# A graph network's first stage: three multiplies for each chunk of edges go from DVE to POOL

## The reference

```
h  = relu(layernorm(x))
xp = h @ W0                               # 3125 x 1024, 4 heads of 256
a_src, a_dst = xp . att_src, xp . att_dst # per node and head
alpha = softmax over the edges of a node (and itself) of leaky_relu(a_src[src] + a_dst[dst])
x  = x + relu(sum over edges of alpha * xp[src] + bias)
h  = relu(layernorm(x));  h = h @ W1;  al = h . a_l;  ar = h . a_r
e  = exp(-leaky_relu(al[src] + ar[dst]))
out = x + elu(sum over edges, by src, of e * h[dst] / (sum of e + 1e-5))
```

## Time and profile before

| | us |
|---|---|
| median of 3 runs | 2025.16 (2017.92 to 2032.6) |
| the profiled execution, its time | 2027.11 |
| its span in the profile | 2025.0 |
| first stage: last scores copied | 503.6 |
| first instruction of the next stage | 513.2 |

### The profile page before, as it was taken

One profiled execution on the slowest core, in us unless ns is written; L12 is line 12 of the kernel. 1 busy time (PEld: TensorE's weight loads), 2 busy tenths in 40 slices (PEclk: granted clock), 3 DMA queues, 4 the chain that ended last, 5 costly groups with the idle time before them and its releaser, 6 DMA issues. The chain is left out here.

```text
span 2025.0 us, 27950 instructions
## 1 busy us (share of the span) xinstructions
PE 1583.1 (78%) x10493; PEld 837.8 (41%) x10493; DVE 1233.0 (61%) x2870; ACT 445.0 (22%) x768; POOL 1039.1 (51%) x1060
## 2 busy tenths in 40 slices
PE   3897999897168777777677676169999999999896
PEld 2444545443034344344344333014544544454454
DVE  4999999997147777777777877342333333333332
ACT  3332333221002221122211221021222221122121
POOL 1121212111656776767767650376666766666630
PEclk9897999998577787878878887569999999999898
DMA  7321333221889999999999983599999999999961
GB/s 234 93 93 57 87 93 96 85 94 48 348 304 347 381 362 382 369 374 381 379 376 373 380 330 113 206 410 352 365 360 359 352 363 355 344 370 349 330 213 47
DMA packets 170575, 554.44 MB, mean 274 GB/s; under 512 B 32195, under 2 KB 37178, under 8 KB 170080
## 3 DMA queue, kind: packets, MB, share of 16 engines
q0 software_dynamic: 128128, 417.93, 56.0%
q1 hardware_dynamic: 38708, 121.44, 17.4%
q10 hardware_dynamic: 3600, 13.24, 1.8%
HBM read 547.51 MB, written 53.52 MB: 297 GB/s over the span
## 5 line engine op out<-in xcount | busy, mean ns | idle before, releaser
L1064 POOL DMA_INDIRECT ring<-layer_rows,idx x360 | 394.4, 1096 | 188.3 <-issue 86.8
L1655 POOL DMA_INDIRECT ring<-layer_rows,idx x360 | 369.7, 1027 | 186.3 <-issue 94.8
L588 PE MATMUL mm<-w_sb,hT 128*128 128x512 f32 x800 | 362.6, 607 | 0.0
L1190 PE MATMUL acc<-ring,weight 128*32 128x256 f32 (+1 forms) x3600 | 334.6, 480 | 26.4 <-issue 14.3
L1717 PE MATMUL acc<-ring,weight 128*32 128x512 f32 x1600 | 221.3, 630 | 39.7 <-issue 34.5
L588 PEld LDWEIGHTS mm<-w_sb,hT 128*128 128x128 f32 x800 | 153.4, 197 | 174.7 <-issue 174.7
L1190 PEld LDWEIGHTS acc<-ring,weight 128*32 128x32 f32 (+1 forms) x3600 | 154.0, 137 | 155.3 <-issue 118.4
L1817 DVE TENSOR_TENSOR hT_low<-tp_l,hT_high 128x512 fp32r<-128x512 f32 x50 | 34.6, 692 | 300.3 <-issue 248.4
L467 POOL CAST row_l<-asd 128x4 bf16<-128x4 f32 x25 | 4.8, 190 | 336.9 <-DVE asd L677 336.9
L1750 PE MATMUL mm_l<-w_high,hT_high 128*128 128x512 f32 x400 | 169.1, 423 | 8.5 <-issue 6.0
L1752 PE MATMUL mm_l<-w_high,hT_low 128*128 128x512 f32 x400 | 163.4, 409 | 10.1 <-issue 10.0
(11 more groups left out here) (271 smaller groups left out, 2419.0 us busy)
## 6 DMA issues: line engine op xcount, KB each, us to landing
layer_rows<-row_l ACTq DMA_DIRECT2D x25, 517.0 KB
layer_rows<-row_l SPq DMA_DIRECT2D x25, 514.0 KB
own<-layer_rows SPq DMA_DIRECT2D x25, 512.0 KB
x<-xb SPq DMA_DIRECT2D x25, 512.0 KB
x1t<-x SPq DMA_DIRECT2D x25, 512.0 KB
xt<-in_x_dram SPq DMA_DIRECT2D x24, 512.0 KB
xb<-in_x_dram SPq DMA_DIRECT2D x24, 512.0 KB
out_dram<-y SPq DMA_DIRECT2D x24, 512.0 KB
```

The source lines that it names most:

```text
L588: last = pe.matmul(mm[k][:, f * HALF:(f + 1) * HALF], hT[k][:, c, :], w_sb[:, c, f * HALF:(f + 1) * HALF], start=c == 0, stop=c == KC - 1)
L1064: pool.indirect_dma_start(out=ring[:, t % 2, blocks(c), :][:, q, :], out_offset=None, in_=table0, in_offset=bass.IndirectOffsetOnAxis(ap=i ...
L1190: last = pe.matmul(acc[t % 2][k * n:(k + 1) * n, h, :], by[:, k, h, :], ring[:, t % 2, blocks(c), h * C:(h + 1) * C][:, k, :], start=c == ...
L1655: pool.indirect_dma_start(out=fetched(t, c)[:, q, :], out_offset=None, in_=table1, in_offset=bass.IndirectOffsetOnAxis(ap=idx, axis=0), bo ...
```

## The change

placed and the two halves of parts are multiplied by POOL. placed is POOL's place_ranks: it waits for the scan of the chunk (scanned) and, for the buffer, for PE's ranks of the chunk two before. The halves are POOL's spread_fields: it waits for at_spot of the chunk (a new semaphore, spotted). DVE, in turn, waits before at_spot until POOL has multiplied both halves of the chunk before (spread_done), since at_spot has one buffer; its waits for placed_done before mine and before the scan were there already and are now waits for POOL. Sizes, types and the results are the same.

```diff
@@ POOL's functions
+            def place_ranks(c):
+
+                pool.wait_ge(scanned, 3 * c + 1)
+                if c >= 2:
+                    pool.wait_ge(ranked, c - 1)
+                pool.tensor_tensor(placed[c % 2][:, :], running[:, :], mine[c % 2][:, :], ALU.mult)\
+                    .then_inc(placed_done, 1)
+
+            def spread_fields(c):
...
+                pool.wait_ge(spotted, c + 1)
+                then(pool.tensor_tensor(parts[k][:, :, 0, :], at_spot[:, :, :], along(high_T[:, cols]), ALU.mult),
+                     halves_done)
+                then(pool.tensor_tensor(parts[k][:, :, 1, :], at_spot[:, :, :], along(low_T[:, cols]), ALU.mult),
+                     spread_done)
@@ POOL's list
+            for c in chunks_of(-1):
+                place_ranks(c)
             for i in range(TILES):
                 for c in chunks_of(i - 3):
                     scatter(c)
+                for c in chunks_of(i - 2):
+                    spread_fields(c)
+                for c in chunks_of(i):
+                    place_ranks(c)
                 split_scores(i)
-            for c in chunks_of(TILES - 3) + chunks_of(TILES - 2) + chunks_of(TILES - 1):
+            for c in chunks_of(TILES - 3):
                 scatter(c)
@@ DVE's rank_chunk
-                if c >= 2:
-                    dve.wait_ge(ranked, c - 1)
-                dve.tensor_tensor(placed[c % 2][:, :], running[:, :], mine[c % 2][:, :], ALU.mult)\
-                    .then_inc(placed_done, 1)
@@ DVE's spread_chunk
+                if c >= 1:
+                    dve.wait_ge(spread_done, c)
                 then(dve.tensor_tensor(at_spot[:, :, :], along(place[:, :], SPAN), across(spots[:, :], SPAN),
-                                       ALU.is_equal), place_math)
-                then(dve.tensor_tensor(parts[k][:, :, 0, :], at_spot[:, :, :], along(high_T[:, cols], SPAN), ALU.mult),
-                     place_math)
-                then(dve.tensor_tensor(parts[k][:, :, 1, :], at_spot[:, :, :], along(low_T[:, cols], SPAN), ALU.mult),
-                     spread_done)
+                                       ALU.is_equal), spotted)
```

More of the change, by code:

```diff
@@ L333, in lists_and_project @@
         spread_done = sem("spread_done")
+        spotted = sem("spotted")
+        halves_done = sem("halves_done")
         packed_done = sem("packed_done")
@@ L471, in split_scores, with along @@
                 then(pool.tensor_copy(parts16[:, :, 2], rest[:, 1, :]), score_split)
+            def place_ranks(c):
[5 more added lines that the diff above has]
+            def spread_fields(c):
+                k = c % 2
+                cols = slice(c * CB, (c + 1) * CB)
+                def along(line):
+                    return line.rearrange("p (b o) -> p b o", o=1).to_broadcast([P, CB, SPAN])
+                pool.wait_ge(spotted, c + 1)
[3 more added lines that the diff above has]
+                     spread_done)
             pool.wait_ge(empty_out, 32)
```

## The result

The change makes the kernel slower: 2097.2 us in the median of 4 runs (2092.0 to 2107.2) against 2028.9 of the kernel before in the same set, a ratio of 1.035 with a 95% interval of 1.029 to 1.041. The forecast was 2078, in a range of 1980 to 2125. The profiled execution has a span of 2094.3 us, 69.3 more than the 2025.0 of the kernel before. The next stage's first instruction comes at 582.6 us instead of 513.2, 69.4 later: all of it is lost in the first stage.

A forecast was written before the change was run, and what follows sets the result against it. DVE was taken to bound the first stage, PE close behind. placed +25.5, tiles spreading two chunks +18.4 and tiles scattering two +8.4 sum to +52 us, giving 2078 us, in a range of 1980 to 2125.

The forecast's parts named there:

- What bounds, and what was removed: First stage: DVE's queue sets each tile's end, PE close behind at 15.65 us; 78.1 us of multiplies leave DVE.
- What POOL's multiplies take: On POOL: 2.0 ns an element, so 3.7 us for placed and 1.45 for each half.
- The lock works both ways: DVE and POOL: a DVE instruction with two inputs in SBUF waits until POOL's multiply is done; decides the sign.
- placed, 28 times: After each scan: DVE pays placed's 3.7 us in full instead of 1.01; 103.6 us, +25.5 with the removal.
- The halves in a tile with one chunk cost nothing: After at_spot and POOL's scatter: halves run from about 123.5 to 126.5, beside the scan, at no cost.
- The double tiles: Tiles spreading two chunks: DVE's second at_spot waits for both POOL halves, 4.6 us, 4 times, 18.4 us.
- Two scatters in a tile: Tiles after those spreading two chunks: halves queue behind the second scatter, placed starts 2.1 us late, 4 times, 8.4 us.
- the lock works one way only: Rival, chance 0.20: POOL's multiplies are stretched instead, DVE loses its 78 us, PE bounds; 45 us less, 1982 us.
- The cheap multiply: Rival, chance 0.12: POOL near its lower bound, placed at 1.9 us; in all -14 us, 2011 us.
- the held scan: Rival, chance 0.12 shared with POOL near its upper bound (2151 us): the scan needs the port, 84 us more, 2162.

The follow-up runs named there:

- placed alone: Against the kernel before, only placed is multiplied by POOL, both halves of parts staying on DVE: ratio 1.0315, 61 us slower.
- the halves alone: Against the kernel before, only the two halves of parts are multiplied by POOL, placed staying on DVE: ratio 1.0079, 15 us slower.
- the kernel that frees DVE of 50 us: Against the kernel before, only the halves on POOL, timed beside the scan, two at_spot buffers, placed on DVE: ratio 0.9964, 7 us faster.
- with PE's waits mended: Halves on POOL beside the scan, placed on DVE, PE's ranks and list turning waiting for at_spot instead of the halves: 0.9906 against the kernel before, 19 us faster.

## Why the prediction was right, and where it was not

**What bounds, and what was removed**: right. DVE set the pace before and after. 78.6 us of its multiplies went (78.1 forecast). A tile with one chunk came to 17.8 us instead of the 16.4 forecast; the next paragraphs say why.

**What POOL's multiplies take**: right. 3576 ns in the median for placed (3.7 forecast), 1.31 us for an undisturbed half (1.45). That is 1.95 to 2.0 ns an element.

**The lock works both ways**: right, and shown. starts is held for 3.44 us beside placed, free with one input in PSUM, and free again when placed lies beside the scan. Before the change only POOL had been seen to wait.

**placed, 28 times**: mechanism right, size 15 us too large. I added 75 us (3.7 less 1.01, 28 times); placed alone cost 61. The multiply is 0.12 us shorter, and bases, or its first 0.2 us, still runs while POOL starts, so 3.2 us are lost where starts is held and 3.4 where bases is (94 us over the 28 chunks), where 3.7 were charged (104). That is 10 of the 15 us; the rest stays open.

**The halves in a tile with one chunk cost nothing**: wrong, and this is the step that failed. I read POOL's queue as one instruction after the other: scatter until 123.42, then a half, when nbias would be long done. But nbias, 128 x 1 elements, is held from before the half's recorded start, while the scatter ahead of it is still at work, until the half's end, as if the half had the port from about when at_spot is done: 28 us over the stage. The three arrangements show that it is the half and not the scatter: 2.1 us with the scatter ahead, 1.24 with the half ahead, 0.16 with the scatter alone. What I said of the scan held: it covers a half without any cost.

**The double tiles**: too dear. (Two chunks are spread in tiles 1, 7, 13 and 19 and scattered in the next ones; the text before the result says 8 and 9 for 7 and 8, which changes no number.) Where two chunks are spread, at_spot waited as forecast for both halves. From the trace after:

```profile
206.20 0.86 DVE L831 TENSOR_TENSOR at_spot<-place,spots 128x672 f16<-128x672 f16 x1
...
208.04 1.83 POOL L492 TENSOR_TENSOR parts<-at_spot,high_T 128x672 f16<-128x672 f16 x1
...
209.95 1.31 POOL L494 TENSOR_TENSOR parts<-at_spot,low_T 128x672 f16<-128x672 f16 x1
211.37 0.86 DVE L831 TENSOR_TENSOR at_spot<-place,spots 128x672 f16<-128x672 f16 x1 [1.47 <-POOL parts L494]
```

The second at_spot begins 4.3 us after the first one's end (4.7 forecast), though only 1.5 us of it are idle time, where I had said about 3. But the tile took 22.1 us, where my terms give 20.22 + 2.69 - 3.56 + 4.6 = 23.95. Two scatters in a tile added 1.3, 0.2, 0.7 and -0.4 us to what a common tile lost, not 2.1 each.

So the terms for the halves gave -50 + 18 + 8 = -23 us, and the halves alone measured +15; placed gave +75 and measured +61. Of the first error, 38 us, nbias is 25, and DVE's waits for the rows, 14 us longer than before, are most of the rest. The second error, -14, partly cancels it. The two kernels don't add up to the change: by their stage ends they lose 63 and 16 us, 79 together, and the change loses 69. With placed on POOL too DVE is late enough to wait only 3.5 us for the rows, not 16, which is about that difference. Forecast +52, measured +68. The sign and the range came from the lock; the closeness of the number is partly luck.

**The rivals.** That the lock works one way only is refuted. Its price is of use still: I took 45 us for DVE freed of its work, and the kernel that frees DVE of 50 us gained 7, with PE's waits mended 19. My sum had PE's work too small and left out its standstills. It gave 389 us for a stage in which PE is busy for 401. And PE stands still in tiles where DVE or POOL is long (37 us in the kernel with the halves beside the scan, 413.9 less 377.1 in 22 tiles, and 40 before), and can't make it up. The cheap multiply and the held scan are refuted by the lengths.

## What to carry to other kernels

Before an instruction goes from DVE to POOL, list which of DVE's instructions POOL can hold: here those that read two tensors from SBUF, and mine, which reads one. While POOL multiplies out of SBUF, the next of them waits until POOL is done, be it on one element for each partition, and that waiting looks like busy time. Here such a move paid only where POOL's work was made to begin with a long DVE instruction that POOL doesn't hold (the scan, with its second operand in PSUM), by a wait that times it. What it may gain is then not the work taken away but what the next engine leaves, read tile by tile with its standstills, and not from its sum.

## What the runs showed of the hardware that was not expected

- POOL's half seems to hold DVE before its start in the trace: with a scatter (1.03 us) ahead of it on POOL, nbias was held from 138.02 although the half is recorded from 138.76; with the scatter alone it ran in 0.16 us. The Trainium skill, GPSIMD Engine Reference, section Instruction dispatch, says that a core of POOL starts the next instruction as soon as it has finished its own share of the one before. If most of the cores have little to do in a scatter, that would fit; which cores worked when, no run here shows.
- An indirect DMA's instruction on POOL, about 1 us, holds no DVE instruction with two inputs in SBUF (nbias 0.16 us, parts 0.86 us beside it), but a multiply on POOL does.
- Who comes first is settled within a tenth of a microsecond, and the recorded starts don't tell it: where bases is recorded 0.10 us ahead of placed it runs free (0.22 us, then starts is held, 3.44), as in most chunks of the changed kernel; recorded 0.04 to 0.06 us ahead, in the kernel with placed alone, it was held in 17 chunks (3.64 us) and ran free in 9. bases and starts together take 3.66 or 3.86 us.
